# A two-block transformer on one core: products behind the second step, silu from tanh, other slots for the fronts, sums on TensorE, other load order

## The chip, the cores and the metric

One core of a Trainium2 chip runs the whole program in one launch. The metric is the device time in microseconds (us) of one execution, as the median of some runs. "PE" is TensorE, "DVE" VectorE, "ACT" ScalarE, "POOL" GpSimd and "SP" SyncE, which here only issues DMAs.

## What is computed

The input is x, 8 batches of 512 rows of 512 numbers in f32. Four sublayers follow one another, each added to x after a layer norm without weights (`ln`):

```python
x = x + ln(attention0(ln(x)))      # 16 heads of 128, 4 key heads, rope, decay instead of softmax
x = x + ln(feed_forward0(ln(x)))   # h = silu(g) * u ; 512 -> 2048 -> 512, integer weights with a scale per row
x = x + ln(attention1(ln(x)))      # 32 heads of 16, 8 key heads, causal softmax
x = x + ln(feed_forward1(ln(x)))   # h0 = the row that all tokens get, from the last token by 4 steps
# feed_forward1: layer_norm(x + sigmoid(x @ gate_w + gate_b) * h0) * gamma + beta
```

In `feed_forward0`, g = (x @ gate_w.T) * gate_scale and u = (x @ up_w.T) * up_scale, 2048 columns each, taken here as 16 pieces of 128.

## The kernel before

**Staging.** The outer loop runs n from 0 to 8. Pass n does the first attention of batch n, then 48 slots, and in the slots the second attention of batch c = n - 1 beside the feed-forward of batch n. Pass 8 has only the second attention of batch 7. Then come short phases on the 8 last rows (one for each batch), and a last stage over 32 tiles of 128x512, which makes the gated sum, its weighted layer norm, the plain layer norm and the residual. A matrix product in near-full precision is three fp32r products of a high and a low half ("hi", "lo"); ACT makes the high half, DVE or POOL the low one.

**Slots.** Slot s is `q, i = divmod(s, 12)`. With i < 8, an even i is a gate product into PSUM bank P0 and an odd i an up product into bank P1; with i of 8 to 11 it is a down product for 128 tokens. From slot 5 on to slot 36 a slot also holds two steps of the second attention (`steps_at`). A step is four banks of scores: transposed scores into the pair T, from which DVE takes the row maxima (a mask addition L1396 and `row_max` L1399), and scores into the pair E, from which ACT takes the exponential (`probs`, L1057). Each pair has no double: PE may fill T again when the maxima of the step before are taken, and E when its exponential is. PE's order in a half slot is transposed scores, half of the feed-forward product, the small transposes of packed queries, keys and maxima, then scores. `spare()` gives these transposes the bank P0 in odd slots and P1 in even ones.

**What follows a product.** ACT takes silu of P0 into `silu` (L1123), which frees P0. DVE multiplies P1, the scale and `silu` into `hf` (L1411), which frees P1, between the slot's two steps. ACT copies `hf` to `hT_hi` at the top of the next even slot, ahead of its exponentials; POOL makes `hT_lo` (L885) from both. DVE also adds down products to `y_acc` (L1422), in slots with i of 8 to 11.

**Fronts.** A front is the input of a batch made ready: DVE normalizes a tile (`xn`, L1201), PE transposes it (L1751), ACT and DVE split it into `XnT_hi` and `XnT_lo` (L1171). Those of batch n + 1 are placed in slots 43 to 46 (`FRONT_X`), in the banks P0 and P1 in turn.

**Loads.** SP issues DMAs in the order of its program, each at its turn. At the start: x of batch 0, eight constants, four raw weight pieces, tables and decay; then the pieces that the host gives in another form are split by ACT (L965) and DVE on the fly in batch 0, and written back in halves for the later batches. PE, ACT and DVE wait once, at the very start, for all eight constants. The ring of 512 KB weight units for batch 1 is refilled after batch 0's last slot (`next_unit` after slot 47).

**Last stage.** For each tile DVE runs eight operations in a fixed, skewed order: gated product L1677, affine L1682, first sum L1687, output sum L1693, two statistics L1658, their aggregation L1663, scaling L1705. ACT has two (L1149, L1156), POOL the reciprocal roots (L929). PE only writes 8 broadcast rows into the 8 banks before it (L2071).

Of the kernel before, what the change touches and what calls it, by code (L numbers as in the profile page):

```python
# [136 lines left out]
MEASURE_X, NORM_X, FRONT_X = 30, 36, 43  # L137
# [108 lines left out]
def build(nc, x, raw_f, raw_i, gate_scale, up_scale, down_scale, rope1_tables, causal, identity_b,  # L246
# [8 lines left out]
    with ExitStack() as ctx:  # L255
# [18 lines left out]
        eps, minus_half = sb("eps", [P, 1]), sb("minus_half", [P, 1])  # L274
# [6 lines left out]
        eps_ffn = sb("eps_ffn", [P, 1])  # L281
# [102 lines left out]
        const_in, act_const_in = sem("s_const_in"), sem("s_identr")  # L384
        pool_const = sem("s_pool_const")
        x_in = [count(f"x_in{n}", NB // 2, step=16) for n in range(2)]
        x2_out, x2_in = count("x2_out", NB, step=16), count("x2_in", NB, step=16)
# [45 lines left out]
        silu_done, h_f, h_hi, h_lo = (count(k, NB, NM) for k in ("silu", "h_f", "h_hi", "h_lo"))  # L433
# [72 lines left out]
        fin_sent = [count(f"fin_sent{n}", NB // FIN_RING + 1, NT, step=16) for n in range(FIN_RING + 1)]  # L506
# [3 lines left out]
        fin_stats, fin_moments = ([count(f"fin_{k}{n}", NF) for n in range(2)] for k in ("stats", "moments"))  # L510
        fin_rstd, fin_shift2 = [count(f"fin_rstd{n}", NF) for n in range(2)], count("fin_shift2", NF)
        BC_BANKS = ("P0", "P1", "T0", "T1", "E0", "E1", "O", "Y0")
# [15 lines left out]
        N_CONST = 16 * 8  # L528
# [3 lines left out]
        def _(sp):  # L532
# [45 lines left out]
            def tokens_in(n):  # L578
                sp.dma_start(X[n % 2][:, :, :], x[n, :, :].rearrange("(t p) d -> p t d", p=P)).then_inc(*x_in[n % 2].hit(n // 2))
# [76 lines left out]
            tokens_in(0)  # L656
            for dst, src in ((ident[:, :], identity), (mask[:, :], causal), (ident_b[:, :], identity_b),
                             (rope1[:, :, :, :].rearrange("p a t d -> p (a t d)"), rope1_tables),
                             (gate_bias[:, :], gate_b.partition_broadcast(P)), (dsc[:, :], down_scale.partition_broadcast(P)),
                             (gsc[:, :], gate_scale), (usc[:, :], up_scale)):  # L660
                sp.dma_start(dst, src).then_inc(const_in, 16)
            for r in range(RAW):
                piece_in(r)
            tables(0)
            decay_in(0, 0)
            for n in range(NB + 1):
                c = n - 1
                if n == 0:
                    first(("pro",))
                if n < NB:  # L670
# [17 lines left out]
                    if n == 0:  # L688
                        first(("ho",))
# [15 lines left out]
                for s in range(SLOTS):  # L705
                    q, i = divmod(s, 12)
                    if n < NB:
                        if n == 0:
                            first(("slot", s))
                            if s == SLOTS - 1:  # L710

                                for slot in range(RING):
                                    sp.wait_ge(*unit_out[slot].need(unit_out[slot].dims[0] - 1))
# [36 lines left out]
                if n == 0:  # L750
                    for k in range(UNITS_A + UNITS_C + 24, UNITS):
                        next_unit(n, k)
# [24 lines left out]
        def _(pool):  # L777
# [3 lines left out]
            pool.wait_ge(pool_const, 3)  # L781
# [53 lines left out]
            for n in range(NB + 1):  # L835
# [24 lines left out]
                if n < NB:  # L860
                    for g in range(KV0):
# [3 lines left out]
                        if g == 1 and c >= 0:  # L865
                            for t in range(NT):
                                rstds("pc", c, t)
                if n < NB:
# [37 lines left out]
            pool.tensor_tensor(pd_shift[:, :], pd_moments[:, :, 0:1].rearrange("p n a -> p (n a)"), pd_rstd[:, :], ALU.mult).then_inc(fin_shift, 1)  # L906

# [1261 lines left out]
```

## Time and profile before

| | us |
|---|---|
| median of 3 runs (lowest, highest) | 4232.41 (4232.01, 4233.1) |
| the profiled execution | 4231.18 |
| its span in the trace | 4229.4 |
| PE busy in the span | 3652.6 (86%) |
| the period of batches 2 to 7 in the slots' loop | about 465 |
| the last stage, 4073.8 to 4229.4 | 155.6 |

The span is the time from the first to the last instruction that the trace shows; 1.8 us of the profiled execution lie around it. A row of the timeline gives start and length in us, and in brackets how long the engine stood idle before and what released it. "PEclk" is the granted clock of PE: 1.00 is 2.4 GHz, 0.50 is 1.2 GHz.

### The profile page before, as it was taken

To read this page: it belongs to the slowest core of one execution; us is meant where nothing else is said; L and a number is where in the kernel's file an instruction comes from. 1 tells how busy PE (TensorE), PEld (TensorE's weight loads), DVE (VectorE), ACT (ScalarE), POOL (GpSimd) and SP (SyncE) were. 2 spreads that over 40 slices of the span, in tenths; PEclk is the share of its full clock that TensorE was granted. 3 is DMA by queue.
4 is the path that set the end of the run, shared out by engine and by line. 5 is a ranking of instruction groups with operands and counts; after the bars stand their busy time and mean duration, and the time that the engine had idled before them with its cause. 6 is when DMAs were issued, how large, how long until landed. Compare 5 with 4: busy or idle time off the path is not lost.

```text
span 4229.4 us, 51038 instructions
## 1 busy us (share of the span) xinstructions
PE 3652.6 (86%) x18024; PEld 2669.3 (63%) x18024; DVE 2536.3 (60%) x4206; ACT 1602.0 (38%) x2364; POOL 1352.8 (32%) x1637
## 2 busy tenths in 40 slices
PE   6878899999999999999999999999999999967640
PEld 4756676577756776577757776677657775643310
DVE  5644567556664666556664666466755666465459
ACT  4422334524253434434353434433452425323112
POOL 2421442235312541245213531244223531211125
PEclk9989999999999999999999999999999999966765
DMA  6456433254324533353325442443325432231213
GB/s 232 169 193 244 159 134 141 77 203 152 127 91 149 176 116 131 122 181 130 143 79 183 140 164 71 174 140 135 140 77 198 155 120 91 99 104 70 110 40 119
DMA packets 173752, 578.98 MB, mean 137 GB/s; under 512 B 14679, under 2 KB 14935, under 8 KB 168126
## 3 DMA queue, kind: packets, MB, share of 16 engines
q1 hardware_dynamic: 169806, 568.37, 37.8%
q10 hardware_dynamic: 3696, 7.34, 0.5%
q8 instruction: 149, 2.44, 0.2%
q14 instruction: 101, 0.83, 0.1%
HBM read 490.19 MB, written 84.93 MB: 136 GB/s over the span
## 4 chain that ended last, share of the span: by engine, by line
PE 62%; DVE 20%; issue 6%; ACT 5%; POOL 4%; DMA 2%; SPq 0%; DVEq 0%; ACTq 0%; POOLq 0%
PE ps_P L1731 24%; PE ps_Y L1731 10%; PE ps_E L1731 6%; PE ps_O L1731 4%; PE ps_O L1917 4%; DVE row_max L1399 3%; PE ps_T L1883 3%; PE ps_T L1731 3%; POOL pT_lo L813 3%; DVE pf L1288 2%; PE ps_E L1901 2%; DVE ps_T L1396 2%; DVE stats L1195 1%; ACT pT_hi L943 1%; DVE stats L1658 1%
## 5 line engine op out<-in xcount | busy, mean ns | idle before, releaser
L1731 PE MATMUL ps_P<-XnT_hi,w_ring 128*128 128x512 f32 x3328 | 1086.2, 408 | 68.8 <-DVE XnT_lo L1171 14.5
L1731 PEld LDWEIGHTS ps_P<-XnT_hi,w_ring 128*128 128x128 f32 x3328 | 611.7, 192 | 255.2 <-issue 99.8
L1731 PE MATMUL ps_P<-XnT_lo,w_ring 128*128 128x512 f32 x1664 | 661.9, 398 | 0.0
L813 POOL TENSOR_TENSOR pT_lo<-pf,pT_hi 128x512 fp32r<-128x512 f32 x320 | 411.4, 1293 | 300.7 <-ACT pT_hi L943 296.1
L1057 ACT ACTIVATE probs<-ps_E 128x1024 f32<-128x1024 f32 (+2 forms) x384 | 339.1, 883 | 422.2 <-PE ps_E L1901 287.9
L831 POOL TENSOR_SCALAR_AFFINE_SELECT probs<-probs 128x512 f32<-128x512 f32 x256 | 163.2, 638 | 990.2 <-ACT probs L1057 989.9
L1399 DVE TENSOR_REDUCE row_max<-ps_T 128x2 fp32r<-128x768 f32 (+3 forms) x384 | 401.9, 1047 | 13.2
L885 POOL TENSOR_TENSOR hT_lo<-hf,hT_hi 128x512 fp32r<-128x512 f32 x128 | 164.6, 1286 | 645.3 <-ACT hT_hi L943 645.3
L1731 PEld LDWEIGHTS ps_P<-XnT_lo,w_ring 128*128 128x128 f32 x1664 | 318.9, 192 | 71.7
L1731 PE MATMUL ps_Y<-w_big,hT_hi 128*128 128x512 f32 x896 | 332.5, 417 | 26.4 <-DVE y_acc L1422 12.6
L804 POOL TENSOR_TENSOR sines<-swapped,sinT 128x512 f32<-128x512 f32 x160 | 214.3, 1340 | 380.2 <-ACT swapped L943 374.1
L1396 DVE TENSOR_TENSOR ps_T<-ps_T,mask 128x256 f32<-128x256 f32 (+1 forms) x384 | 198.4, 517 | 203.8 <-PE ps_T L1883 199.9
L943 ACT ACTIVATE pT_hi<-pf 128x512 fp32r<-128x512 f32 x320 | 202.1, 632 | 312.1 <-DVE pf L1288 308.5
L1288 DVE TENSOR_TENSOR pf<-ps_T,dec 128x512 f32<-128x512 f32 x320 | 219.6, 690 | 137.2 <-POOL pT_lo L813 104.8
L1883 PE MATMUL ps_T<-KT,QT 64*128 64x128 f32 (+3 forms) x1024 | 188.8, 402 | 110.5 <-DVE row_max L1399 107.5
L943 ACT ACTIVATE swapped<-ps_P 64x512 f32<-64x512 f32 x320 | 189.8, 593 | 242.5 <-PE ps_P L1731 133.3
L1731 PEld LDWEIGHTS ps_Y<-w_big,hT_hi 128*128 128x128 f32 x896 | 169.3, 189 | 105.7 <-issue 28.2
L1883 PEld LDWEIGHTS ps_T<-KT,QT 64*128 64x128 f32 x1024 | 95.1, 193 | 220.2 <-DVE row_max L1399 126.2
L1411 DVE SCALAR_TENSOR_TENSOR hf<-ps_P,usc,silu 128x512 f32<-128x512 f32 x128 | 95.9, 749 | 192.3 <-PE ps_P L1731 189.2
L1901 PE MATMUL ps_E<-QT,KT 64*128 64x512 f32 (+2 forms) x768 | 164.0, 412 | 54.6 <-ACT probs L1057 53.5
L1223 DVE TENSOR_TENSOR roped<-ps_P,cosT 128x512 f32<-128x512 f32 x160 | 110.3, 689 | 141.8 <-ACT swapped L943 141.8
L1917 PE MATMUL ps_O<-probs,V 128*32 128x512 f32 (+3 forms) x2048 | 182.9, 480 | 0.0
(285 smaller groups left out, 7099.4 us busy)
## 6 DMA issues: line engine op xcount, KB each, us to landing
w_ring<-split_dram SPq DMA_DIRECT2D x412, 512.0 KB, 3.4
w_big<-split_dram SPq DMA_DIRECT2D x64, 2048.0 KB, 7.7
dec<-decay SPq DMA_DIRECT2D x32, 1024.0 KB, 4.9
split_dram<-w_ring SPq DMA_DIRECT2D x58, 512.0 KB, 4.3
split_dram<-w_big SPq DMA_DIRECT2D x36, 512.0 KB, 4.3
wo1w<-split_dram SPq DMA_DIRECT2D x8, 2048.0 KB, 7.7
gatew<-split_dram SPq DMA_DIRECT2D x7, 2048.0 KB, 9.9
X<-x SPq DMA_DIRECT2D x8, 1024.0 KB, 10.6
```

Source lines behind the costliest of these rows:

```text
L804: pool.tensor_tensor(sines[:, u % 2, :], swapped[:, u % 2, :], sinT[:, :], ALU.mult)\
L813: pool.tensor_tensor(pT[1][:, k % 4, :], pf[:, k % 2, :], pT[0][:, k % 4, :].bitcast(F32), ALU.subtract).then_inc(*p_lo.hit(n, g, k))
L885: pool.tensor_tensor(hT[1][:, m % IC, :], hf[:, m % 2, :], hT[0][:, m % IC, :].bitcast(F32), ALU.subtract).then_inc(*h_lo.hit(n, m))
L943: return act.activation(out_, in_, ACT.Copy)
L1057: act.activation(probs[j][:, m, :].rearrange("p (b n) i -> p b n i", n=nh), psE[:, :, 0:nh * w].rearrange("p b (n i) -> p b n i", i=w), AC ...
L1288: dve.tensor_tensor(pf[:, k % 2, :].rearrange("p (h i) -> p h i", h=HG), ps[TB[k % 2]][:, :].rearrange("p (h i) -> p h i", h=HG), dec[:, : ...
L1396: dve.tensor_tensor(corner, corner, mask[:, :].unsqueeze(1).unsqueeze(1).to_broadcast([P, 2, nh, P]), ALU.add)\
L1399: dve.reduce_max(row_max[:, g % 2, i_, m].rearrange("p (b n) -> p b n", n=nh), src, AX_X)\
L1731: last = pe.matmul(dst, stat[s_], mov[m_], start=first_ and k == 0, stop=last_ and k == n - 1)
L1883: mm = pe.matmul(dst[half][:, m * w:(m + 1) * w], QT[rows_, g % 3, pair, cols(b)], KT[rows_, g % 3, 0:w], start=True, stop=True)
L1901: pe.matmul(dst[half][:, 0:nh * w].rearrange("p (h i) -> p h i", i=w), KT[rows_, g % 3, cols(j)], QT[rows_, g % 3, pair:pair + nh, j * P:S ...
L1917: last = pe.matmul(dst[at:at + 32, j * P:S], V1[:, j, g, :], probs[j][:, m, :], start=(j == 0), stop=(j == NT - 1), skip_group_check=True)
```

## The change

1. **Order on DVE.** In slots with i < 8, `product_out` stands behind the slot's second step; with i of 8 to 11 it stays between the two.
2. **silu.** ACT writes tanh(g / 2) instead of silu(g), by a scale `ghalf` = gate_scale / 2. A new DVE operation computes (tanh + 1) * P0 and now frees P0. `ughalf` = up_scale * gate_scale / 2 takes the rest, since g * sigmoid(g) = (g / 2)(1 + tanh(g / 2)). With this ACT's program has 18 table loads instead of 145.
3. **Fronts.** Slots 42 to 45, banks T0, T1, P0, P1; the split halves follow in slots 44, 44, 45, 46.
4. **Waits of PE.** A pair of banks freed by one event is waited for once, not twice (`fill_both`).
5. **Last stage.** PE makes both sums as f32 products with the identity, in the banks E0, E1 and O, Y0; the broadcast rows use P0, P1, T0, T1, four at a time. DVE keeps six of eight operations for a tile, ACT gets the shifts as bias and one copy more, POOL one small multiplication more.
6. **Loads.** x of batch 0 comes in four tiles with a semaphore each, the identity after the first tile; seven constants come after the first attention's loads, and PE, ACT and DVE wait for them later. Four pieces of V weights move from the opening to the units of the first group, one for each; the decay goes behind the opening. Batch 1's first ring units are issued one by one in slots 36 to 43 of batch 0.

```diff
@@ slots of the fronts, opening pieces
-MEASURE_X, NORM_X, FRONT_X = 30, 36, 43
+FRONT_X, HALVES_X, BANKS_X = (42, 43, 44, 45), (44, 44, 45, 46), ("T0", "T1", "P0", "P1")
-    out = {("pro",): [("u", j) for j in range(RING)] + [("w", BIG_V, k) for k in range(4)]}
+    out = {("pro",): [("u", j) for j in range(RING)]}
-                out["p", g, u] = [("u", NU * g + u + RING)]
+                out["p", g, u] = [("u", NU * g + u + RING)] + ([("w", BIG_V, u)] if g == 0 and u < 4 else [])
@@ SP
-            tokens_in(0)
-            for dst, src in ((ident[:, :], identity), (mask[:, :], causal), (ident_b[:, :], identity_b),
...
-            for r in range(RAW):
+            for t in range(NT):
+                sp.dma_start(X[0][:, t, :], x[0, t * P:(t + 1) * P, :]).then_inc(*x0_in[t].hit(0))
+                if t == 0:
+                    sp.dma_start(ident[:, :], identity).then_inc(ident_in, 16)
+            for r in range(2):
                 piece_in(r)
             tables(0)
-            decay_in(0, 0)
+            for r in range(2, RAW):
+                piece_in(r)
...
+                            if q == NQ - 1 and i < 8:
+
+                                k = UNITS_A + UNITS_C + 8 * q + i
+                                slot = slot_of[0, k]
+                                sp.wait_ge(*unit_out[slot].need(unit_out[slot].dims[0] - 1))
+                                next_unit(n, k)
@@ ACT, slots and last stage
-                        act.activation(silu[:, m % 2, :], ps["P0"][:, :], ACT.Silu, scale=gsc[:, m:m + 1])\
-                            .then_inc(*silu_done.hit(n, m))
+                        act.activation(silu[:, m % 2, :], ps["P0"][:, :], ACT.Tanh, scale=ghalf[:, m:m + 1])\
+                            .then_inc(*tanh_done.hit(n, m))
...
+            def fin_copy(k):
+                act.wait_ge(*fin_back.need(k))
+                copy(fin_place(k)[1], ps[OUT_BANKS[k % 2]][:, :]).then_inc(*fin_out.hit(k))
@@ DVE, slots
-                if i < 8 and i % 2:
+                if i < 8 and i % 2 == 0:
+                    m = 4 * q + i // 2
+                    dve.wait_ge(*tanh_done.need(n, m))
+                    dve.scalar_tensor_tensor(silu[:, m % 2, :], silu[:, m % 2, :], 1.0, ps["P0"][:, :], ALU.add, ALU.mult)\
+                        .then_inc(*silu_done.hit(n, m))
+                elif i < 8:
...
-                    if n < NB:
+                    if n < NB and s % 12 >= 8:
                         product_out(n, s)
                     if c >= 0:
                         for i in steps[1:]:
                             step(c, i)
+                    if n < NB and s % 12 < 8:
+                        product_out(n, s)
@@ PE, pairs of banks and last stage
-                dst = [fill(TB[half], max_done.need(c, g, x_)) for half in range(2)]
+                dst = fill_both(TB, max_done.need(c, g, x_))
...
+            for k in range(NF + FIN_SKEW):
+                if k < NF:
+                    pe.wait_ge(*fin_h_done.need(k))
+                    pe.wait_ge(*fin_gated.need(k))
+                    dst = fill(SUM_BANKS[k % 2], fin_scaled.need(k))
+                    pe.matmul(dst[:, :], ident[:, :], fin_h[:, k % 4, :], start=True, stop=False)
+                    pe.matmul(dst[:, :], ident[:, :], fin_place(k)[1], start=False, stop=True).then_inc(*fin_sum.hit(k))
+                old = k - FIN_SKEW
+                if 0 <= old < NF:
+                    x3_, z = fin_place(old)
+                    pe.wait_ge(*fin_w.need(old))
+                    dst = fill(OUT_BANKS[old % 2], fin_out.need(old))
+                    pe.matmul(dst[:, :], ident[:, :], x3_, start=True, stop=False)
+                    pe.matmul(dst[:, :], ident[:, :], z, start=False, stop=True).then_inc(*fin_back.hit(old))
+                if k < NF and k % NT == NT - 1 and k // NT + 4 < NB:
+                    fin_row(k // NT + 4)
```

On DVE, in slots 12 and 13 of a batch (the mask addition and the maxima are a step's two operations; QT is a copy of packed queries from the spare bank), before:

```order
L1350 CAST QT<-ps_P0 128x512
L1396 TENSOR_TENSOR ps_T<-ps_T,mask 128x2x128
L1399 TENSOR_REDUCE row_max<-ps_T 128x2
L1411 SCALAR_TENSOR_TENSOR hf<-ps_P1,usc,silu 128x512
L1396 TENSOR_TENSOR ps_T<-ps_T,mask 128x2x128
L1399 TENSOR_REDUCE row_max<-ps_T 128x2
```

and after, at the same place:

```order
L1450 SCALAR_TENSOR_TENSOR silu<-silu,ps_P0 128x512
L1392 CAST QT<-ps_P0 128x512
L1438 TENSOR_TENSOR ps_T<-ps_T,mask 128x2x128
L1441 TENSOR_REDUCE row_max<-ps_T 128x2
L1438 TENSOR_TENSOR ps_T<-ps_T,mask 128x2x128
L1441 TENSOR_REDUCE row_max<-ps_T 128x2
L1460 SCALAR_TENSOR_TENSOR hf<-ps_P1,ughalf,silu 128x512
```

`hf` stands one step later, and the new operation on P0 stands at the end of the even slot, ahead of the copy that reads what PE next puts in P0.

On ACT, over the same slots and the next, before:

```order
L943 ACTIVATE KT<-ps_Y0 128x512
L943 ACTIVATE hT_hi<-hf 128x512
L1057 ACTIVATE probs1<-ps_E 128x2x384 x2
L943 ACTIVATE q_pack<-R_q 128x16x32
L943 ACTIVATE k_pack<-R_k 128x16x16
L1123 ACT_TABLE_LOAD
L1123 ACTIVATE silu<-ps_P0,gsc 128x512
L1057 ACT_TABLE_LOAD
L1057 ACTIVATE probs2<-ps_E 128x1024
```

and after:

```order
L972 ACTIVATE KT<-ps_Y0 128x512
L972 ACTIVATE hT_hi<-hf 128x512
L1086 ACTIVATE probs1<-ps_E 128x2x384 x2
L972 ACTIVATE q_pack<-R_q 128x16x32
L972 ACTIVATE k_pack<-R_k 128x16x16
L1156 ACTIVATE silu<-ps_P0,ghalf 128x512
L1086 ACTIVATE probs2<-ps_E 128x1024
```

The two table loads are gone; the copy `hT_hi` keeps its place ahead of the exponentials.

On PE, in the last stage, where nothing but the broadcast rows stood before, there is now for each tile (and a broadcast row after every fourth):

```order
L2132 MATMUL ps_E<-fin_h,ident 128x512
L2133 MATMUL ps_E<-fin_z,ident 128x512
L2139 MATMUL ps_O<-fin_x,ident 128x512
L2140 MATMUL ps_O<-fin_z,ident 128x512
L2122 MATMUL ps_P1<-rows,ident 128x512
```

Four products of 128x512 in f32 for a tile are new on PE.

## Rows read from the trace of the kernel before

**Rows 1.** The page: busy time of each engine, its share of the span, instructions.

```profile
PE 3652.6 (86%) x18024; PEld 2669.3 (63%) x18024; DVE 2536.3 (60%) x4206; ACT 1602.0 (38%) x2364; POOL 1352.8 (32%) x1637
```

**Rows 2.** By stretch: its ends, length, busy us of PE, PEld, DVE, ACT, POOL; clock.

```profile
2048.70:2304.20 255.50, 232.91 (x1297) 161.49 (x1296) 148.97 (x255) 106.83 (x139) 55.65 (x76) 0.99 0.37 133
4073.80:4229.40 155.60, 8.74 (x14) 2.96 (x12) 150.59 (x288) 40.34 (x60) 78.69 (x160) 0.51 0.30 108
```

**Rows 3.** Groups of PE in the slots of batch 4: busy, mean ns, idle before.

```profile
L1883 PE MATMUL ps_T<-KT,QT 64*128 64x128 f32 (+3 forms) x128 | 22.6, 386 | 9.4 <-DVE row_max L1399 9.2
L1901 PE MATMUL ps_E<-QT,KT 64*128 64x512 f32 (+2 forms) x96 | 19.5, 392 | 6.4 <-ACT probs L1057 6.2
```

**Rows 4.** Timeline: start, length, instruction, idle before; opening, and the step into batch 1.

```profile
9.76 0.69 DVE L1195 BATCH_NORM_STATS2 stats<-X 128x6 f32<-128x512 f32 x1 [9.76 <-DMA usc<-up_scale]
...
35.09 0.63 ACT L965 ACTIVATE w_big<-raw_a 128x512 fp32r<-128x512 f32 x1 [1.29 <-DMA raw_a<-raw_f]
...
36.97 0.63 ACT L965 ACTIVATE w_big<-raw_b 128x512 fp32r<-128x512 f32 x1 [1.25 <-DMA raw_b<-raw_f]
...
446.22 1.19 PE L1731 MATMUL ps_P<-XnT_hi,w_ring 128*128 128x512 f32 x2 [9.19 <-issue]
```

**Rows 5.** Timeline of slots 0 and 1 of batch 4, ScalarE and VectorE.

```profile
2050.26 1.28 ACT L1123 ACT_TABLE_LOAD   x1 [5.07 <-PE ps_P L1731]
...
2054.37 0.74 DVE L1411 SCALAR_TENSOR_TENSOR hf<-ps_P,usc,silu 128x512 f32<-128x512 f32 x1
```

**Rows 6.** Timeline of slots 13 and 14 of batch 4.

```profile
2112.63 0.75 DVE L1411 SCALAR_TENSOR_TENSOR hf<-ps_P,usc,silu 128x512 f32<-128x512 f32 x1
...
2113.46 0.62 ACT L943 ACTIVATE hT_hi<-hf 128x512 fp32r<-128x512 f32 x1
...
2113.98 0.80 ACT L1057 ACTIVATE probs<-ps_E 128x768 f32<-128x768 f32 x1
2113.99 1.23 DVE L1399 TENSOR_REDUCE row_max<-ps_T 128x2 fp32r<-128x1024 f32 x1
...
2115.72 0.42 PE L1901 MATMUL ps_E<-QT,KT 64*128 64x384 f32 x2
```

**Rows 7.** Timeline of slot 28 of batch 4: a table load and PE's wait.

```profile
2214.92 1.28 ACT L1057 ACT_TABLE_LOAD   x1
2216.21 0.81 ACT L1057 ACTIVATE probs<-ps_E 128x768 f32<-128x768 f32 x1
...
2217.17 0.44 PE L1901 MATMUL ps_E<-QT,KT 64*128 64x384 f32 x2 [2.14 <-ACT probs L1057]
```

**Rows 8.** Timeline of the end of batch 4: the waits of its fronts.

```profile
2293.89 0.66 PE L1751 MATMUL ps_P<-ident,xn 128*128 128x128 f32 x4 [1.16 <-DVE xn L1201]
...
2302.72 0.74 PE L1731 MATMUL ps_P<-XnT_hi,w_ring 128*128 128x512 f32 x2 [2.18 <-DVE XnT_lo L1171]
```

**Rows 9.** Timeline of the last stage: its opening, one period of VectorE, its end.

```profile
4072.59 1.98 PE L2071 MATMUL ps_P<-rows,ident 32*128 32x512 f32 x4 [0.77 <-DVE rows L1646]
...
4074.41 1.87 PE L2071 MATMUL ps_T<-rows,ident 32*128 32x512 f32 x4
...
4078.92 1.91 PE L2071 MATMUL ps_O<-rows,ident 32*128 32x512 f32 x2
...
4094.59 0.68 DVE L1677 TENSOR_TENSOR fin_z<-ps_P,fin_z 128x512 f32<-128x512 f32 x1
4095.19 0.74 DVE L1682 SCALAR_TENSOR_TENSOR fin_z<-fin_z,rstd,y_acc 128x512 f32<-128x512 f32 x1
...
4099.27 0.68 DVE L1677 TENSOR_TENSOR fin_z<-ps_P,fin_z 128x512 f32<-128x512 f32 x1
...
4226.18 0.75 DVE L1693 SCALAR_TENSOR_TENSOR y<-y,var_eps,xr 128x512 f32<-128x512 f32 x1 [1.53 <-ACT y L1156]
```

**Rows 10.** By stretch again, two of the short row phases; the clock stands third last.

```profile
4002.40:4005.00 2.60, 2.60 (x16) 0.63 (x20) 0.00 (x0) 0.00 (x0) 0.00 (x0) 0.50 1.05 388
4005.00:4012.00 7.00, 4.73 (x46) 1.46 (x42) 1.38 (x2) 3.84 (x6) 0.00 (x0) 1.00 0.20 71
```

More of the change, by code:

```diff
@@ L381, in raw, with tokens_at @@
             return (raw_a if r % RAW < 2 else raw_b)[:, r % 2, :]
-        const_in, act_const_in = sem("s_const_in"), sem("s_identr")
+        const_in, act_const_in, ident_in = sem("s_const_in"), sem("s_identr"), sem("s_ident_in")
+        x0_in = [count(f"tile{t}", 1, step=16) for t in range(NT)]
         pool_const = sem("s_pool_const")
         x_in = [count(f"x_in{n}", NB // 2, step=16) for n in range(2)]
+        def tokens_at(n):
+            return n // 2 - (n % 2 == 0)
         x2_out, x2_in = count("x2_out", NB, step=16), count("x2_in", NB, step=16)
@@ L432, in build @@
         gate_mm, up_mm = count("gate_mm", NB, NM), count("up_mm", NB, NM)
-        silu_done, h_f, h_hi, h_lo = (count(k, NB, NM) for k in ("silu", "h_f", "h_hi", "h_lo"))
+        tanh_done, silu_done, h_f, h_hi, h_lo = (count(k, NB, NM) for k in ("tanh", "silu", "h_f", "h_hi", "h_lo"))
+        scales = sem("s_scales")
         down, down_acc = count("down", NB, NQ, NT), count("down_acc", NB, NQ, NT)
@@ L505, in build @@
         fin_in = [count(f"fin_in{n}", NB // FIN_RING + 1, step=32) for n in range(FIN_RING)]
-        fin_sent = [count(f"fin_sent{n}", NB // FIN_RING + 1, NT, step=16) for n in range(FIN_RING + 1)]
+        fin_sent = [Count(s_.sem, NB // FIN_RING + 1, NT, step=16, after=1) for s_ in x0_in]
         fin_bc, fin_shift = count("fin_bc", NB), sem("s_fin_shift")
@@ L509, in build @@
         fin_gated, fin_sum, fin_scaled, fin_affine, fin_out = (count("fin_" + k, NF) for k in ("gated", "sum", "scaled", "affine", "out"))
[L510 to L512 removed]
+        fin_stats = [count(f"fin_stats{n}", NF) for n in range(2)]
+        fin_moments, fin_rstd = ([Count(s_[k].sem, NF, after=NB * NT) for k in ("xa", "pa")] for s_ in (ln_moments, ln_rstd))
+        fin_back = count("fin_back", NF)
+        fin_shift2 = count("fin_shift2", NF)
+        BC_BANKS, SUM_BANKS, OUT_BANKS = ("P0", "P1", "T0", "T1"), ("E0", "E1"), ("O", "Y0")
         def fin_place(k):
@@ L669, in _ @@
                     first(("pro",))
+                    decay_in(0, 0)
                 if n < NB:
@@ L1663, in fin_aggregate @@
                 dve.bn_aggr(moments[:, n, :], stats[:, n, :]).then_inc(*fin_moments[m].hit(k))
-            dve.wait_ge(fin_shift, 1)
-            for k in range(NF + FIN_SKEW):
-                new, mid, old = k, k - 1, k - FIN_SKEW
+            for k in range(NF + 2):
+                new, mid, old = k, k - 1, k - 2
                 if new < NF:
@@ L1717, in fill, with fill_both @@
                 return ps[bank]
+            def fill_both(banks, emptied):
+                if banks[0] in empties:
+                    pe.wait_ge(*empties[banks[0]])
+                    if empties[banks[1]] != empties[banks[0]]:
+                        pe.wait_ge(*empties[banks[1]])
+                empties[banks[0]] = empties[banks[1]] = emptied
+                return [ps[bank] for bank in banks]
             def unit_ready(n, k):
@@ L1895, in scores_T @@
                     pe.wait_ge(*m_in[g % 2].need((c * KV1 + g) // 2))
-                dst = [fill(EB[half], exp_done.need(c, g, x_)) for half in range(2)]
+                dst = fill_both(EB, exp_done.need(c, g, x_))
                 for half, heads in enumerate(sets):
```

159 lines of the change are left out of this document (86 added, 73 removed).

## The prediction

> **What bounds the kernel now.** I read the page first: PE is busy for 3652.6 us of 4229.4, DVE for 2536.3 [rows 1]. The busy time by stretch says where this average hides two regimes. In the slots of a middle batch PE is busy for 232.91 of 255.50 us at a granted clock of 0.99, with DVE at 148.97 and ACT at 106.83; in the last stage DVE is busy for 150.59 of 155.60 us and PE for 8.74, at 0.51 [rows 2]. So the slots are worth only PE's gaps, 22.6 us a batch, and there a delayed engine costs only when PE comes to wait for it. The groups show what it waits for: 9.4 us ahead of transposed scores for the maxima, 6.4 us ahead of scores for the exponentials [rows 3]. Last I read timelines: the opening and the step into batch 1 [rows 4], slots [rows 5 to 7], the fronts [rows 8], the last stage [rows 9].
>
> **Opening, -10 (-15 to -5).** DVE's first statistics and ACT's identity wait until 9.76 for the last constant [rows 4]. Now the first tile and the identity suffice: I take -4.4, between 0 (x's four tiles arrive no sooner) and -6. Four V pieces leave the opening; two that follow each other stand at 35.09 and 36.97 [rows 4], so four are 4 x 1.9 = -7.5. They and the 1 MB decay now contend in the first group's units, where each unit splits two pieces; at one piece each, I give back +2 (0 to +7).
>
> **Batch 0's slots, +6 (0 to +15).** ACT and DVE split weights there beside the products, so 16 more operations of 0.75 us on DVE (the price of `hf`, [rows 6]) are 12 us if each comes before PE's next use of P0, nothing if none does. I take half, and for the top 3 us more of queueing.
>
> **Step into batch 1, -12 (-13 to -9).** PE stands 9.19 us ahead of its first product and waits for what SP loads after slot 47 [rows 4]. With units issued eight slots earlier the wait goes; about 3 us more come from the products behind it, which ran at half clock (the first two in 1.19 us instead of the 0.74 of [rows 8]). SP's other DMAs in those slots are passed by short issues; if one blocks on a unit still in use, this is only postponed and the gain falls to the lower bound.
>
> **Slots of batches 1 to 7, +8.2 a batch, +57 (-25 to +75).** This is the term on which all hangs, so each place by itself.
> - Slot 0: PE wants P0 for slot 2 one product after the table load at 2050.26, about 2052.9 (12 matmuls of 512 columns, at 2.4 GHz 0.213 us each). DVE reaches its product only at 2054.37, behind the rotations [rows 5]. Before, silu on ACT came right behind the load and freed P0 in time. The new operation starts at 2054.37 and ends 0.75 later: P0 is free at 2055.1, +2.2.
> - Slot 7 and 8: the packed queries need P0 behind the new operation, which now follows two steps, +1.2; the down products need the last `hT_lo`, 1.29 us on POOL behind a later `hf`, +1.6.
> - Slots 14, 18, 20, 26 and 30: `hf` ran at 2112.63 between the steps. Behind the second step's maxima (1.23 us from 2113.99) it ends at about 2115.9 instead of 2113.4. ACT's copy (0.62) stands ahead of the next exponential (0.80), which would end at 2117.3 instead of 2114.8; PE took the bank pair E again at 2115.72 [rows 6]. That is 1.6 here less what the pipeline absorbs; by the same working the five places give 1.8, 2.1, 1.8, 1.8 and 1.3, together +8.8. Queued behind the waiting copy are the exponentials, and PE waits for those.
> - Gains: a layout one step earlier in slot 6, -0.7. Two table loads of 1.28 us stand between products and exponentials in the worst slots; the wait of 2.14 behind one [rows 7] and a like one of 1.57 go, -3.7. The other of the nine loads in a batch's slots lie in ACT's idle time and are worth nothing. One wait less per pair, which I estimate at 0.05 us on the 25 or so that block, -1.2.
>
> The sum is 2.2 + 1.2 + 1.6 + 8.8 - 0.7 - 3.7 - 1.2 = +8.2, and seven batches give +57. Where both operations fall into DVE's waits for PE and ACT's copy finds `hf` done, only the gains stay: -5.6 a batch, of which I keep -3.6 (-25 in all) as the low end. The high end adds 2.5 a batch for stalls that push the next ones.
>
> **The Trainium skill, "ScalarE: Activation LUTs", section "What ACT_TABLE_LOAD costs"**, gives about 1283 ns for the load and some 1380 ns more for a drain at each switch. The load agrees with this trace; the drain doesn't: the exponential starts at 2216.21, where the load that began at 2214.92 ends [rows 7]. By the page's 2.66 us a switch those two places would give up to 2.8 us more a batch, 19 us in all.
>
> **Fronts, -20 (-23 to -8).** PE waits 1.16 us for `xn` and 2.18 us for the last `XnT_lo` before batch 5's first product [rows 8]. With the transposes a slot earlier and four banks, two down products cover the second; the last low half (0.69 us) and `xn` are then long done. Six boundaries by 3.3 = -20. If T0 and T1 are still held by rows of the output, half of it stays.
>
> **Pass 8, -3 (-8 to 0)**: there PE has no feed-forward between the steps and waits at nearly each pair, so only the single waits give something, 60 or so by 0.05.
>
> **Last stage, -23 (-32 to -12).** DVE's period is 4.68 us a tile (4094.59 to 4099.27), one of its eight operations 0.60 (to 4095.19) [rows 9]. Two sums at 0.66 leave 3.35. PE now has four f32 products a tile. Two broadcast rows of the same 512 columns take 1.82 us at full clock (4072.59 to 4074.41) and their bare length is 0.86 each; at half clock two took the 1.71 apiece that the row at 4078.92 begins with [rows 9]. So PE needs 4 x 0.86 = 3.44, a quarter of a broadcast row 0.21, and 0.1 for waits: 3.75, and becomes the bound. ACT has three operations of 0.7, POOL stays at 78.69 / 32 = 2.5 plus 0.2 [rows 2]. 32 x 3.75 = 120 against 150. The chain behind the last tile (shift, ACT, PE, ACT's copy) is 3 us longer than now, where the last DVE operation starts at 4226.18 [rows 9]; the first tiles cost another 3 to 5 at half clock. -30 + 3 + 4 = -23.
>
> **Sum.** -10 + 6 - 12 + 57 - 20 - 3 - 23 = -5. Against the profiled execution, 4231.2, this is 4226; it lies 1.2 under the median of the runs, so I say 4227.
>
> **Rivals.**
>
> *The stalls don't bite.* For it: PE's gaps total only 22.6 us a batch, DVE is idle for 0.4 of the slots [rows 2], and its new operations would fall into pauses that end when PE delivers. A stall also delays PE's next request, so five stalls need not cost five times. Against it: the exponential at 2113.98 has 0.9 us to spare before PE's 2115.72, and `hf` moves by 2.5. With -3.6 to +4 a batch instead of +8.2 the time is 4227 - 30 to 4227 - 83: 4144 to 4197, with 4185 as its middle if half bites.
>
> *The slower side: the last stage stays at half clock.* The granted clock there is 0.51 [rows 2], PE does nothing now in long pauses, and the products begin cold. At 1.71 each a tile takes 4 x 1.71 + 0.43 = 7.3 us; it decides as soon as a product takes more than (4.68 - 0.3) / 4 = 1.1 us. Then the stage is 32 x 7.3 = 233 instead of 127: about 4320. Against it: in the row phases, which are f32 products too, 16 of PE's instructions without a pause stood at 0.50 and those that follow at 1.00 [rows 10], and PE would be busy without pause once it is the bound. The Trainium skill, "TensorE: Matmul & The Clock Gate", section "What's actually happening", says the same of cause, a throttle that activity releases; its "Part 4: PE-mode transpose" says that a transpose doesn't count as activity the same way. These are plain products with an identity; if they counted as transposes do, this rival would hold.
>
> *The stalls bite harder, or batch 0 does.* DVE's and ACT's queues in fixed order pass a delay on to the next slot. At +11 a batch and +15 in batch 0 the time is 4227 + 20 + 9 = 4256.
>
> *The change doesn't do what it says*: DVE in the last stage waits for PE's banks in turn, four latencies in a ring of two, and the period stays near 4.7. Then only 5 of the 23 us are lost or won: 4245. Its chance is in the slower cases.
>
> **How the numbers follow.** The sum as worked out (4212 to 4242): 0.42, of which 0.13 lie under 4224. Stalls that don't bite or bite half: 0.31. Harder stalls, or a last stage without gain: 0.18, of which a little falls within. Half clock at the end: 0.09. The range leaves out the half clock and the lowest part of the first rival: 4172 to 4262. Less than 0.2%, 8.5 us, can't be told from no change in this kernel; faster than 4224: 0.44, within: 0.25, slower than 4241: 0.31. The likeliest case's own range is 4212 to 4242.
>
> **What would show it.** Right: PE idle in a middle batch's slots near 31 us, with the group of scores waiting for `probs` up from 6.4 to about 13 and ACT's `hT_hi` waiting longer for `hf`; no wait ahead of the first product of a batch; PE busy without pause in the last stage at clock 1.00, tiles 3.75 us apart. Wrong: a last stage at 0.50; PE's waits in the slots unchanged, which would bring the first rival; or products of batch 0 that wait on DVE for P0.

## The result and the profile after

| | before | after |
|---|---|---|
| median, us (lowest, highest; 20 runs each) | 4228.26 (4218.36, 4237.4) | 4240.07 (4228.71, 4263.18) |
| ratio of the runs, with its 95% interval | | 1.0034 (1.0022 to 1.0045) |
| the profiled execution, its span | 4231.18, 4229.4 | 4233.51, 4231.7 |

The change makes the kernel slower by 0.34%, some 14 us by the ratio and 11.8 by the medians, where 5 us faster was forecast. The profiled execution of before is on the slow side of its runs and that of after on the fast side, so the two traces differ by only 2.3 us.

I cut both traces at the same marks: the first product of slot 0 of batch 0, the first cosine product (`roped`) of batch 1 on DVE, the last down product of batch 7, the first broadcast row of the last stage, and the end.

| stretch | before ends at | after ends at | after less before, us | prediction |
|---|---|---|---|---|
| opening and first attention of batch 0 | 255.1 | 255.9 | +0.8 | -10 |
| slots of batch 0, step into batch 1 | 453.1 | 446.3 | -7.6 | -6 |
| batches 1 to 7 | 3696.4 | 3723.6 | +34.0 | +37 |
| pass 8 and row phases | 4072.6 | 4094.0 | -5.8 | -3 |
| last stage | 4229.4 | 4231.7 | -19.1 | -23 |

First the page of after, against [rows 1], then the busy time by stretch: the slots of batch 4 and the last stage, against [rows 2] (ends, length, busy PE, PEld, DVE, ACT, POOL; third last the granted clock).

```profile
PE 3787.2 (89%) x18280; PEld 2720.6 (64%) x18280; DVE 2571.8 (61%) x4270; ACT 1459.4 (34%) x2269; POOL 1335.1 (32%) x1674
```

```profile
2057.50:2320.70 263.20, 238.95 (x1305) 164.34 (x1303) 159.16 (x271) 83.66 (x121) 54.44 (x74) 0.97 0.35 127
4098.00:4231.70 133.70, 121.63 (x264) 50.18 (x262) 108.04 (x222) 61.27 (x92) 63.51 (x192) 0.96 0.35 126
```

The first of them begins with the first product of slot 0. The row of before in [rows 2] begins 1.4 us behind that product; from the same mark it is this one:

```profile
2047.30:2304.20 256.90, 234.31 (x1304) 162.63 (x1303) 150.34 (x258) 106.83 (x139) 55.65 (x76) 0.99 0.37 133
```

The batch's slots are 6.3 us longer, but PE's gaps there are 24.3 us against 22.6 of before: only 1.7 more. The other 4.6 us are busy time of PE on nearly the same work, at a clock of 0.97 instead of 0.99. The last stage has turned over as forecast: PE is busy for 121.63 of 133.70 us, at 0.96.

The groups of PE in the slots of batch 4, against [rows 3]:

```profile
L1933 PE MATMUL ps_T<-KT,QT 64*128 64x128 f32 (+3 forms) x128 | 23.3, 401 | 6.0 <-DVE row_max L1441 5.5
L1951 PE MATMUL ps_E<-QT,KT 64*128 64x512 f32 (+2 forms) x96 | 18.8, 387 | 9.6 <-ACT probs L1086 9.6
```

Waits for the maxima fell from 9.4 to 6.0 us, and waits for the exponentials rose from 6.4 to 9.6. The timeline of slots 13 and 14 of batch 4 after, against [rows 6], shows the second of these:

```profile
2128.42 0.74 DVE L1460 SCALAR_TENSOR_TENSOR hf<-ps_P,ughalf,silu 128x512 f32<-128x512 f32 x1
...
2129.19 0.63 ACT L972 ACTIVATE hT_hi<-hf 128x512 fp32r<-128x512 f32 x1 [2.34 <-DVE hf L1460]
...
2129.73 0.79 ACT L1086 ACTIVATE probs<-ps_E 128x768 f32<-128x768 f32 x1
...
2130.57 0.44 PE L1951 MATMUL ps_E<-QT,KT 64*128 64x384 f32 x2 [1.49 <-ACT probs L1086]
```

ACT waits 2.34 us for `hf` at the head of its queue, the exponential comes after the copy, and PE waits 1.49 us for it. This is the stall that the prediction described, at its place. What it did not price stands right behind. The same execution by stretch, before, in and after the next few us:

```profile
2128.00:2132.00 4.00, 2.27 (x13) 1.39 (x12) 2.55 (x4) 2.25 (x4) 1.30 (x2) 1.00 0.12 50
2132.00:2135.50 3.50, 3.50 (x27) 2.35 (x27) 1.52 (x4) 1.40 (x3) 0.60 (x1) 0.51 0.42 140
2135.50:2139.00 3.50, 3.13 (x19) 2.00 (x18) 3.37 (x5) 1.41 (x2) 0.63 (x1) 1.00 0.06 19
```

PE was busy for 2.27 of 4 us, and then its granted clock fell from 1.00 to 0.51 while it was busy without a pause, and rose again. Counted in the trace's record of the clock, in the slots of batches 1 to 7, before has 12 such stretches with 41.0 us at 1.2 GHz, after has 23 with 92.2 us, 19 of them 3.41 us long and four 6.83. In before eleven of the twelve follow waits of 1.6 to 2.1 us behind a table load, as in [rows 7]; in after they follow the new waits of 1.2 to 2.3 us.

### The profile page after: what moved, and what is told of

It reads as the page before. It is cut to its first block and busy times, and to the rows that moved or that the text cites. A ratio compares the mean times of both kernels' runs of the same rounds, so it can differ in the third digit from the quotient of the medians.

```text
span 4231.7 us, 50932 instructions
## 1 busy us (share of the span) xinstructions
PE 3787.2 (89%) x18280; PEld 2720.6 (64%) x18280; DVE 2571.8 (61%) x4270; ACT 1459.4 (34%) x2269; POOL 1335.1 (32%) x1674
## 5 line engine op out<-in xcount | busy, mean ns | idle before, releaser
L1781 PE MATMUL ps_Y<-w_big,hT_hi 128*128 128x512 f32 x896 | 340.6, 425 | 36.3 <-POOL hT_lo L910 17.5
L1156 ACT ACTIVATE silu<-ps_P,ghalf 128x512 f32<-128x512 f32 x128 | 87.7, 685 | 308.2 <-PE ps_P L1781 308.2
L972 ACT ACTIVATE hT_hi<-hf 128x512 fp32r<-128x512 f32 x128 | 80.8, 631 | 327.8 <-DVE hf L1460 327.7
```

The source lines that it names most:

```text
L972: return act.activation(out_, in_, ACT.Copy)
L1781: last = pe.matmul(dst, stat[s_], mov[m_], start=first_ and k == 0, stop=last_ and k == n - 1)
```

## The experiments

Theory 1 was that the order on VectorE is what costs: it makes waits of PE of more than a us, and beside the wait itself the clock falls after it. The rivals were that stretches at half clock come by chance, that the added operation on P0 is what costs, and that neither the clock nor the order matters. Ratios are to the kernel before on the same chip; "slots" is the mean length of the slots of batches 1 to 7, from the first product of slot 0 to the first products of the next batch; "waits" are PE's idle time for each batch in the slots of batches 1 to 7, "half clock" the time at 1.2 GHz in all of them.

| run | median, us | ratio (95%) | slots, us | waits | half clock |
|---|---|---|---|---|---|
| before | 4224.81 | | 257.2 | 22.4 | 41.0 |
| e1 changed again | 4244.38 | 1.0039 (1.0027 to 1.0052) | 261.6 | 24.3 | 78.5 |
| e2 up product between | 4139.73 | 0.9803 (0.979 to 0.9816) | 249.1 | 17.6 | 6.8 |
| e3 high half later | 4166.61 | 0.9862 (0.9847 to 0.9877) | 252.4 | 19.1 | 27.3 |
| e4 the same, first product early | 4144.48 | 0.9806 (0.9793 to 0.982) | 249.7 | 17.5 | 10.2 |
| e5 filled waits | 4204.46 | 0.9948 (0.9936 to 0.9961) | 258.0 | 15.7 | 13.7 |
| e6 up between, first early | 4126.26 | 0.9766 (0.9753 to 0.9779) | 246.9 | 15.9 | 0.0 |
| e7 loads alone | 4213.45 | 0.997 (0.9959 to 0.9982) | 257.6 | 22.4 | 51.2 |
| e8 silu, up between | 4165.65 | 0.9857 (0.9842 to 0.9872) | 252.6 | 18.8 | 37.5 |
| e9 order alone | 4311.81 | 1.0197 (1.0181 to 1.0213) | 268.2 | 29.7 | 81.9 |
| e10 loads and last stage | 4202.85 | 0.994 (0.9924 to 0.9956) | 258.0 | 22.4 | 58.0 |
| e11 both and high later | 4131.61 | 0.977 (0.9755 to 0.9786) | 247.0 | 15.9 | 0.0 |
| e12 filled pass 8 | 4133.31 | 0.9781 (0.9768 to 0.9794) | 246.9 | 15.9 | 0.0 |

The first line is before's median beside e1 to e4, its slots, waits and clock from its trace. Beside e5 to e8 before stood at 4226.85, beside e9 to e11 at 4225.52, beside e12 at 4226.91.

### The order on VectorE and ScalarE

**e1**, the changed kernel again, has no edit.

> The changed kernel, unaltered, timed beside the others, as the point that they are compared with. Theory 1 (added waits of PE of 1.2 to 2.3 us, after which the granted clock falls to 0.50 for 3.4 us at a time): between 15 and 30 such stretches in the slots of batches 1 to 7, a ratio of 1.002 to 1.005. Theory 2 (such stretches come by chance, and the one profile caught many): nearer to the 12 of the kernel before, and a ratio near 1.000.

It gave 1.0039, with 21 stretches at half clock. So the many stretches are the kernel's, not one execution's.

**e2** puts up products back between the steps:

```diff
-                    if n < NB and s % 12 >= 8:
+                    if n < NB and (s % 12 >= 8 or s % 2):
                         product_out(n, s)
...
-                    if n < NB and s % 12 < 8:
+                    if n < NB and s % 12 < 8 and s % 2 == 0:
                         product_out(n, s)
```

> The changed kernel, but VectorE takes up products (hf, odd slots) between a slot's two steps as before; gate products stay behind the second step. Theory 1: ScalarE's copy hT_hi finds hf done, PE's waits for probs fall from 9.6 us a batch to about 3, the waits of 1.5 to 1.8 us go and with them most stretches at half clock (to 5 to 12); waits for the maxima rise from 5.8 to about 9. Net about 3 us a batch less waiting and 15 us less at half speed: 25 to 40 us faster than the changed kernel, about 4205. Theory 2: the waits even out, the stretches at half clock stay, 4235 to 4240. Theory 3 (the added operation on P0 is the cost, not the order): 4235 or more.

4139.73, 105 us under e1, is far more than the 25 to 40 expected. The groups of batch 4:

```profile
L1933 PE MATMUL ps_T<-KT,QT 64*128 64x128 f32 (+3 forms) x128 | 22.6, 389 | 8.0 <-DVE row_max L1441 7.5
L1951 PE MATMUL ps_E<-QT,KT 64*128 64x512 f32 (+2 forms) x96 | 18.6, 380 | 2.2 <-ACT probs L1086 2.2
L972 ACT ACTIVATE hT_hi<-hf 128x512 fp32r<-128x512 f32 x16 | 10.1, 631 | 24.3 <-DVE hf L1460 24.3
```

The waits for `probs` fall from 9.6 to 2.2 us, those for the maxima rise by 2.0. Over seven batches 6.7 us less waiting are 47 us, and 72 us less at half clock are worth some 36, together 83; the slots as a whole are 12.5 shorter, 87 us. The expectation had the sign of each row, and lost on sizes: it had put the net of the waits at 3 a batch. The two profiled spans differ by 85 us; the rest of the 105 lies in how far each profiled run was from its median.

**e3** leaves VectorE's order and moves ScalarE's copy instead, which is its next in line:

```diff
-                    if n < NB and i in (2, 4, 6, 8):
+                    def high():
                         m = 4 * q + i // 2 - 1
...
+                    late = n < NB and i in (2, 4, 6) and c >= 0 and len(steps_at(s)) > 1
+                    if n < NB and i in (2, 4, 6, 8) and not late:
+                        high()
...
-                        for i_ in steps_at(s):
+                        for j, i_ in enumerate(steps_at(s)):
                             step(c, i_)
+                            if late and j == 0:
+                                high()
```

> The changed kernel, but in slots with i of 2, 4 and 6 ScalarE copies hT_hi behind the first step's exponential, not ahead of it; VectorE's order stays as changed. Theory 1: the exponential no longer queues behind a copy that waits for hf; probs waits fall to 3 us a batch or less, the waits for the maxima stay at 5.8, half-clock stretches fall to 5 to 12: 4190 to 4205, 35 to 50 us faster than the changed kernel. Rival (the second exponential then queues instead, or hf waits for its buffer): no gain, 4235.

4166.61: 78 us under e1, with `hf` as late as in the change (`high` is the copy). So most of the cost is not the place of `hf` as such, but the exponential that queues behind the copy that waits for it. Waits for `probs` fell to 3.7, not below 3; that the exponential of the second step now queues a little is likely, and not shown.

**e4** adds to e3 the first gate product ahead of the last two rotations:

```diff
                     for t in range(NT):
+                        if t == 2 and n < NB:
+                            product_out(n, 0)
                         rotate_pairs(c, 1, t)
...
-                    if n < NB and s % 12 < 8:
+                    if n < NB and s % 12 < 8 and (s or c < 0):
```

> As the run before, and besides VectorE takes the first gate product of a batch (the new operation of slot 0) after two of the four last rotations, not behind all. Theory 1: the wait of 2.30 us a batch in slot 2 goes, and the stretch at half clock that follows it in three of seven batches: 16 us of waiting and 3 to 5 of clock, about 20 us faster than the run before. Rival (PE then waits for the rotations instead, in the packed queries): within 5 us of the run before.

4144.48, 22 us less, as expected. The wait in slot 2 was this one in the changed kernel:

```profile
2065.41 0.70 PE L1781 MATMUL ps_P<-XnT_hi,w_ring 128*128 128x512 f32 x2 [2.29 <-DVE silu L1450]
```

and 0.58 us of it are left. **e6** joins e2 and this edit.

```diff
-                    if n < NB and s % 12 < 8:
+                    if n < NB and s % 12 < 8 and s % 2 == 0 and (s or c < 0):
                         product_out(n, s)
```

> Both moves on VectorE at once: up products between the two steps as before, and the first gate product of a batch ahead of the last two rotations. From the run with the first move (4140) the wait of 2.30 us a batch goes, 0.58 stays: 7 x 1.7 = 12 us, and no clock, since hardly a stretch at half clock is left there: about 4128. Rival (the rotations are late instead): 4140.

4126.26: the fastest, 2.3% under before. In its slots the clock doesn't fall once.

**e9** is part 1 alone, on the kernel before:

```diff
-                    if n < NB:
+                    if n < NB and s % 12 >= 8:
                         product_out(n, s)
...
+                    if n < NB and s % 12 < 8:
+                        product_out(n, s)
```

> The kernel before with part 1 alone: up products (hf) behind a slot's second step; silu, fronts, loads and last stage as before. Theory 1 (this order is what costs the gain, with or without tanh): ScalarE's copy waits for hf, the exponential behind it, and the clock falls after each: 70 to 110 us slower than before, 4295 to 4335, with over 25 stretches at half clock in the slots. Rival (the order only harms beside the new operation on P0): within 20 us of before, 4225 to 4245.

4311.81, 86 us slower, in the middle of theory 1's range. With silu on ScalarE and without the operation on P0, the order alone costs nearly as much as in the changed kernel. The groups of its batch 4, against [rows 3]:

```profile
L1886 PE MATMUL ps_T<-KT,QT 64*128 64x128 f32 (+3 forms) x128 | 23.2, 397 | 6.9 <-DVE row_max L1399 6.6 <-issue 0.2
L1904 PE MATMUL ps_E<-QT,KT 64*128 64x512 f32 (+2 forms) x96 | 19.5, 395 | 13.6 <-ACT probs L1057 13.6
L943 ACT ACTIVATE hT_hi<-hf 128x512 fp32r<-128x512 f32 x16 | 10.1, 633 | 43.7 <-DVE hf L1411 43.7
```

`probs` goes from 6.4 to 13.6. The stretches at half clock were 23, a few short of the expected 25. Of the 11.0 us by which a batch's slots are longer, 7.3 are waits, and 41 us more at half clock in seven batches are worth nearly 3.

**e11** adds e3's edit to e6:

```diff
+                            if late and j == 0:
+                                high()
```

> The fastest kernel so far (4126: up products between, first gate product early) and besides ScalarE's copy hT_hi behind the first step's exponential. Where hf is early, waits for probs are 2.2 us a batch; if the copy is their cause they go: 7 x 2 = 14 us, 4112. If they come from the exponentials' own length: 4126.

Nothing: 4131.61, the same waits of 2.2 us. Where `hf` is early, the copy is in nobody's way.

### Is it the clock, or only the wait?

**e5** changes no wait. It gives PE work in the longest ones, into the bank Y0, which nothing holds there:

```diff
+            def filler(count_):
+                pe.wait_ge(*empties["Y0"])
+                for _ in range(count_):
+                    pe.matmul(ps["Y0"][:, :], identr[:, :], XnT[0][:, 0, :], start=True, stop=True)
...
+                if filling:
+                    filler(5)
```

> The changed kernel, with products on PE whose result nothing reads, placed ahead of its longest waits in batches 1 to 7: five of 512 columns before the scores of slots 14, 18, 20, 26 and 30, eight before the gate product of slot 2. Nothing else moves, and the waits are as long as before, only that PE works in them. Theory 1 (a wait of over a us brings the granted clock down for 3.4 us, which costs beyond the wait): time at half clock in the slots falls from 80 to 90 us to 20 to 40, and the kernel is 15 to 30 us faster though it does more, about 4218. Rival (the stretches at half clock have another cause, or cost nothing): the time stays at 4240 or rises by up to 20 us, what the added products cost where they don't fit the wait.

4204.46, 40 us faster than e1 by the medians and 38 by the ratios, with 231 products more. Batch 3 by stretch, first the changed kernel run again, then with filled waits:

```profile
1579.00:1845.60 266.60, 243.33 (x1304) 167.31 (x1303) 158.86 (x271) 83.68 (x121) 54.56 (x74) 0.96 0.34 125
```

```profile
1572.00:1831.80 259.80, 244.73 (x1337) 168.52 (x1337) 158.73 (x271) 83.66 (x121) 54.51 (x74) 0.99 0.35 128
```

33 instructions more, 6.8 us shorter, clock 0.99 instead of 0.96. ScalarE still waits 46.1 us for `hf` in batch 4, as in e1. The wait and its price in clock are thus two things, and the second is real: in the slots some 25 us of the 40. Another 9 us of the two traces' difference lie in pass 8, which the edit doesn't touch and whose clock varies: before, e7 and e9 have the same program there, and 225, 201 and 222 us of it at half clock.

The 20 runs of the changed kernel fit this without an edit: the slowest, 4263.18, had a mean granted clock of 0.946, the fastest, 4228.71, one of 0.955. That is 0.009 of 4240 us, 38 us of clock, for 34 us of time; over all 20 the time falls as the clock rises, with a correlation of -0.97.

The Trainium skill, "TensorE: Matmul & The Clock Gate", section "What's actually happening", calls it a throttle that the engine's activity releases; e5 agrees, with 78.5 us at half clock before the filling and 13.7 with it.

**e12** carries this to pass 8, where e6 stands at 0.69 for 110 us:

```diff
+                if n == NB and i is not None and quad2(i):
+                    filler(2)
                 if i is not None and quad2(i):
                     scores_T(c, i)
```

Here `filler` makes f32 products of the identity and 256 columns of a table, into P1.

> The kernel at 4126, and in pass 8, where PE has no feed-forward beside the steps and stands at a granted clock of 0.69 for 110 us, two f32 products of 256 columns that nothing reads ahead of each step's scores, about 0.9 us at full clock. Theory 1 carried on (PE's pauses bring the clock down, work in them holds it): clock near 1.00 from 3680 to 3870 and the pass 10 to 25 us shorter, 4101 to 4116. Rival (the products stand in the chain of mask, maxima and scores, which no clock shortens): the clock rises and the time doesn't, 4126 to 4150.

4133.31: the time of the rival. First e6, then e12, from the first maxima of pass 8 to the last, and PE's wait for the maxima in them:

```profile
3663.70:3805.90 142.20, 98.44 (x534) 53.51 (x534) 92.72 (x140) 51.23 (x71) 15.86 (x25) 0.69 0.17 60
```

```profile
L1935 PE MATMUL ps_T<-KT,QT 64*128 64x256 f32 (+3 forms) x124 | 28.5, 498 | 43.6 <-DVE row_max L1441 43.4
```

```profile
3663.60:3819.10 155.50, 131.99 (x687) 77.41 (x688) 92.97 (x140) 50.64 (x70) 15.65 (x25) 0.86 0.16 55
```

```profile
L1935 PE MATMUL ps_T<-KT,QT 64*128 64x256 f32 (+3 forms) x124 | 24.9, 438 | 24.4 <-DVE row_max L1441 24.4
L1943 PE MATMUL ps_P<-rope,ident 128*128 128x256 f32 x155 | 49.7, 448 | 0.0
```

The clock rose to 0.86 and the waits for the maxima fell by 19 us, but the added products took 49.7, and the steps as a whole 13.3 us more. The waits were too short for what was put in them, so the products themselves held the steps up. Whether a higher clock without this would have shortened them, as theory 1 has it, or not, as the rival has it, e12 doesn't show. A filled wait helped where PE has a backlog and the products fit the wait.

### The other parts

**e8** is e2 with silu on ScalarE, and its table loads, instead of tanh and the operation on P0:

```diff
-                        act.activation(silu[:, m % 2, :], ps["P0"][:, :], ACT.Tanh, scale=ghalf[:, m:m + 1])\
-                            .then_inc(*tanh_done.hit(n, m))
+                        act.activation(silu[:, m % 2, :], ps["P0"][:, :], ACT.Silu, scale=gsc[:, m:m + 1])\
+                            .then_inc(*silu_done.hit(n, m))
```

> The run with up products between the steps (4140), but with silu on ScalarE as before, so without the added operation on VectorE and with the table loads. It tells what tanh gives where the order does no harm. If the loads cost the waits of 1.6 and 2.1 us twice a batch and the clock after them: 26 us of waiting and 10 to 15 us of clock, less 16 us for the wait in slot 2 that silu on ScalarE doesn't have: 4160 to 4170. If the added operation costs as much as the loads: 4140.

4165.65, 26 us over e2 by the medians and 23 by the ratios: tanh is worth this much where the order does no harm. Half clock is back at 37.5 us, behind the waits for the table loads.

**e7** is part 6 alone, on the kernel before, the whole of it as in the change; its core:

```diff
-                    for k in range(UNITS_A + UNITS_C + 24, UNITS):
-                        next_unit(n, k)
...
+                if n == 0:
+                    first(("pro",))
+                    decay_in(0, 0)
```

> The kernel before with part 6 alone (tiles and constants, V pieces, decay, batch 1's units). What the prediction said: -10 for the opening, -12 for the step into batch 1, 4203. What the trace of the changed kernel says: the first attention of batch 0 ends only 1 us earlier though it begins 13 us earlier, since the pieces of weights set its pace, and batch 1 begins 7 us earlier: 4225 less 8 = about 4217.

4213.45, 13 us under before. In its trace slot 0 begins 3.1 us earlier and batch 1 begins 11.3 us earlier, against the +0.8 and -6.8 of the changed kernel. **e10** adds part 5, again as in the change; its core on PE:

```diff
+                    pe.matmul(dst[:, :], ident[:, :], fin_h[:, k % 4, :], start=True, stop=False)
+                    pe.matmul(dst[:, :], ident[:, :], fin_place(k)[1], start=False, stop=True).then_inc(*fin_sum.hit(k))
```

> The run with the loads alone (4213) and besides part 5, the sums of the last stage on PE. By the trace of the changed kernel, where the last stage takes 137.7 us from its first broadcast row to the end instead of 156.8: 19 us less, 4194. By the prediction's term, 23 less: 4190. Rival (part of the gain comes from what the other parts leave behind, such as a clock already high): 4200 or more.

4202.85, 11 us less, short of the 19 to 23. But from the first broadcast row to the end its trace takes 138.6 us, against 156.8 in e7: the stage gives 18, as in the changed kernel, and the whole shows 7 less. Two of its six runs, 4194.8 and 4193.82, show all of it, the rest stood at a lower clock (0.956 to 0.959 instead of 0.960). In which stretch, and what moved that clock, is open.

## Why the prediction was wrong, point by point

Three steps of it failed. The opening was to give 10 us and gave none: the prediction asked what the moved V pieces cost the units and not who needs them next, and took the late constants as free. The clock was put at nothing in the slots, where it cost some 25 us; the sum of that term came out near all the same, by luck, since PE's added waits stayed 26 us below the forecast. And the clock of one execution was taken as given, which leaves 10 to 12 us between traces and medians. Point by point:

- **Opening, -10: failed, +0.8.** PE's wait of 13.11 us there did shrink to 5.58. But 20 us later stands a wait that wasn't there:

```profile
28.89 1.19 PE L1781 MATMUL ps_P<-XnT_hi,w_ring 128*128 128x512 f32 x2 [5.58 <-DVE roped L1265]
```

```profile
48.00 0.79 PE L1781 MATMUL ps_Y<-w_big,XnT_hi 128*128 128x512 f32 x1 [8.62 <-DVE w_big L1213]
```

  The V product needs the four V pieces, which now come one by one. The second group's first product starts at 86.4 instead of 88.8: of 12.8 us 2.4 are left. The text gave the pieces back +2 (0 to +7) and asked only what the units cost, not who needs V next. The last fronts of batch 0 then wait 11.5 instead of 8.3 us for `xn`, and this row stands ahead of them:

```profile
235.68 0.22 POOL L890 TENSOR_TENSOR ghalf<-gsc,half 128x16 f32<-128x16 f32 x1 [11.49 <-DMA usc<-up_scale]
```

  POOL waits for constants that part 6 moved behind the first attention, since part 2 makes `ghalf` from them, and its reciprocal roots for these fronts come after that. e7 has the same loads without `ghalf`: its first root there starts at 230.87 instead of 236.42, its fronts wait 8.3 us, and slot 0 begins 3.1 us earlier than in before. By these rows the two parts together cost some 3 us that the loads alone don't; no run moved `ghalf` to test it.
- **Batch 0's slots and the step into batch 1, +6 and -12: right** in the sum, -7.6. The 9.19 us are gone. e7, with the new loads and without the new operation on VectorE, has -8.2 there: the step gave less than 12, and the operation cost less than 6.
- **Slots and fronts, +57 and -20: +34, right in the sum by two errors.** The places came as worked out: +2.29 in slot 2 (2.2 forecast), 1.24 for `hT_lo` (1.6), 1.49 to 1.78 at four of the five slots and 1.10 at the last, together 7.4 (8.8); the packed queries waited 0.2 (1.2). But the waits for the maxima, put at no change, fell by 3.4. Likely this is because the mask of the second step no longer stands behind `hf`: they fall in e9 too, and rise again in e2. So PE's waits rose by 1.6 us a batch in the mean and not by the 5.3 that follow from +57 and -20 over seven batches: 26 us less than forecast. The clock was put at nothing: 51 us more at half clock, some 25 us in all, 3.6 a batch. The prediction used the clock for the last stage alone; at the waits of 1.6 to 2.1 us of the kernel before, whose trace already had the clock falling behind them, it did not look. Its own sign of being right, PE idle near 31 us and the group of `probs` near 13, was not met: 24.3 and 9.6.
- **From -5 to +14.** Between the two traces the miss is 7 us: opening +11, batch 0 -2, last stage +4, batches -3, pass 8 -3. The other 10 to 12 us stand between traces and medians: the profiled run of before was 3 us over its median, that of after 7 under, at a clock of 0.953 where the slow ones had 0.946 to 0.950. The forecast took one execution's clock as given, in a change that adds waits after which the clock may fall.
- **Fronts: partly.** The wait for `XnT_lo` is gone, that for `xn` is 1.4 instead of 1.16 in batch 4: -1.9 instead of -3.3.
- **Pass 8, -3: -5.8.** Not tested apart. Before, e7 and e9 have the same program there and take 376.2, 366.5 and 374.2 us, so -5.8 can't be told from the spread.
- **Last stage, -23: -19.1, right in kind.** PE is the bound, products of 0.86 us, with a period of 3.44 us where nothing disturbs:

```profile
4149.53 1.02 PE L2132 MATMUL ps_E<-fin_h,ident 128*128 128x512 f32 x2
...
4152.97 1.02 PE L2132 MATMUL ps_E<-fin_h,ident 128*128 128x512 f32 x2
```

  Over 31 tiles it is 3.86, forecast 3.75, since PE waits for tiles that come late and spent 11 us at half clock. The rival of a stage at 1.2 GHz didn't come true; its own numbers, 4227 and 233 instead of 127, give 4333 and not 4320.
- **The rival in which the stalls don't bite** was wrong in kind: they bite at nearly every place named. In size it was nearer than the sum: without the fronts PE's waits rose by 3.5 us a batch, inside its -3.6 to +4, and the clock took the gain back. The slower rival with a time near 4256 had the side right, with a wrong cause.

## What to carry to other kernels

An operation moved to a later place in one engine's queue is priced at the queue of the engine that waits for it: here one copy waited, and the exponential behind it cost PE 1.1 to 1.8 us five times a batch. Moving either the producer (e2) or the copy (e3) takes most of that away, and with it the change is 2.0% or 1.4% faster instead of 0.3% slower. Where PE has a backlog, a wait of a us or two can cost twice, once by itself and once by the clock after it; price both from the trace, and see where the clock already falls in the kernel before. When a load is put off, look for every engine that waits for it, here POOL too.

## What the runs showed of the hardware that I had not expected

- The stretches at 1.2 GHz inside a batch that is otherwise at 2.4 are 3.41 us long, a few 6.83, and behind the same waits they come in some batches and not in others: in the profiled execution of the changed kernel six in batch 3, none in batch 6. The changed kernel spreads over 34 us in 20 runs and the one before over 19 in 20; e6, without such stretches, over 5 in 4 runs, but e3, with 27.3 us of them, over 3 in 4, so that they make the whole spread isn't shown.
- Work whose result nothing reads made a kernel faster: e5, 40 us by the medians, in waits that held it.
- POOL's reciprocal root in the last stage takes 564 ns instead of the 933 ns of before, though its form is the same; DVE is busy there for 108 of 134 us instead of 151 of 156. The cause was not tested.

```profile
L956 POOL TENSOR_TENSOR rstd<-var_eps,minus_half 128x1 f32<-128x1 f32 x64 | 36.1, 564 | 5.0
```
